# A graph layer's edge loop: first radial layer of two groups on two row groups of TensorE, and edge attributes copied by ScalarE into free columns of PSUM

## The reference

```python
h = jnp.maximum(_layernorm(x, axis=-1), 0.0)          # 6250 nodes x 160
l0, l1 = _fctp_scalar_attr(x0, x1, a, W_l1_0, W_l1_1)  # node table, gathered by src
r = jax.nn.relu(edge_length_embedded @ W_fc1 * (1.0 / np.sqrt(N_BASIS))) * RELU_GAIN  # 206250 x 10 -> 100
w = r @ W_fc2 * (1.0 / np.sqrt(N_RADIAL))              # -> w0 64, w1 64, w2 32, w3 32
y0 = l0[edge_src]; y1 = l1[edge_src]
e0 = edge_attr[:, :1]; e1 = edge_attr[:, 1:4]
m0 = w0 * y0 * e0
m1 = (w1 * y0)[:, :, None] * e1[:, None, :]
m2 = (w2 * e0)[:, :, None] * y1
m3 = w3 * jnp.einsum('eud,ed->eu', y1, e1) * INV_SQRT3
# sums of m0..m3 over the edges of each dst (sorted), W_l2_*, plus the node's own part, plus x
```

## Time and profile before

| | |
|---|---|
| median of 3 runs | 2946.77 us (2910.21 to 2948.76) |
| profiled execution | 2931.67 us |
| its span, first to last instruction | 2929.9 us |
| mean granted TensorE clock | 0.749 |
| TensorE matmuls busy | 2518.0 us |
| VectorE busy | 1661.1 us |
| GpSimd busy | 1617.6 us |
| ScalarE busy | 340.0 us |

### The profile page before, as it was taken

The page is one execution under the profiler, slowest core; times in us unless marked ns, Lnnn a source line. Parts: engine busy times, 40 slices in busy tenths (PEclk is TensorE's granted clock), DMA queues, the critical chain, the costliest instruction groups (busy, mean ns, idle before and its releaser), DMA issues.

```text
span 2929.9 us, 41982 instructions
## 1 busy us (share of the span) xinstructions
PE 2518.0 (86%) x11466; PEld 2003.8 (68%) x11466; DVE 1661.1 (57%) x4639; ACT 340.0 (12%) x636; POOL 1617.6 (55%) x1637
## 2 busy tenths in 40 slices
PE   6889888788989988888888888898888889898888
PEld 6667776667767766666666666676676677676677
DVE  5455656556656556555655555565565556556555
ACT  5000111011101011010101101010110111011111
POOL 4645555555655555545555554555465555555553
PEclk8566778787767687877777777777778777677876
DMA  4212222222222222212222221222122222222221
GB/s 132 58 45 52 54 55 54 51 53 53 56 50 55 53 52 56 52 47 55 50 53 50 54 55 48 52 51 56 46 60 51 50 52 54 50 55 52 51 53 36
DMA packets 160622, 158.30 MB, mean 54 GB/s; under 512 B 87570, under 2 KB 132534, under 8 KB 160602
## 3 DMA queue, kind: packets, MB, share of 16 engines
q0 software_dynamic: 77376, 132.16, 18.3%
q1 hardware_dynamic: 82088, 24.49, 3.7%
q10 hardware_dynamic: 1138, 1.43, 0.1%
HBM read 149.90 MB, written 8.03 MB: 54 GB/s over the span
## 4 chain that ended last, share of the span: by engine, by line
PE 57%; another core or an unknown queue 15%; DVE 13%; issue 10%; DVEq 4%; ACT 1%; DMA 0%; POOL 0%; ACTq 0%; SPq 0%; POOLq 0%
PE ps_w L894 16%; PE ps_s L922 14%; PE ps_s L924 12%; PE ps_h L887 11%; DVE hot L686 3%; DVEq L745 2%; DVE acc L742 2%; DVE dot L661 2%; DVE dots L656 2%; DVE msg L677 1%; DVE hot L680 1%; PE ps_s L910 1%; DVEq L742 1%; PE ps_s L906 1%
## 5 line engine op out<-in xcount | busy, mean ns | idle before, releaser
L381 POOL DMA_INDIRECT y<-table,idx x1612 | 1583.6, 982 | 1274.2 <-DVE msg L677 657.4
L894 PEld LDWEIGHTS ps_w<-w_fc,hr 100*128 100x128 f32 x3224 | 682.8, 241 | 456.9 <-issue 404.2
L894 PE MATMUL ps_w<-w_fc,hr 100*128 100x192 f32 x3224 | 839.2, 417 | 49.2 <-issue 26.8
L922 PE MATMUL ps_s<-hot,msg 128*128 128x128 f32 x3216 | 612.8, 346 | 136.5 <-DVE msg L677 84.9
L922 PEld LDWEIGHTS ps_s<-hot,msg 128*128 128x128 f32 x3216 | 569.3, 255 | 180.6 <-DVE msg L677 111.8
L742 DVE TENSOR_TENSOR acc<-acc,ps_s 64x32 f32 (+1 forms) x1612 | 327.1, 203 | 628.8 <-remote 346.7
L887 PE MATMUL ps_h<-rad,w_fc 10*100 10x512 f32 x806 | 556.8, 775 | 80.0 <-ACT hid_t L492 43.4
L924 PE MATMUL ps_s<-hot,msg 128*128 128x64 f32 x3216 | 531.6, 314 | 88.1 <-issue 87.7
L924 PEld LDWEIGHTS ps_s<-hot,msg 128*128 128x128 f32 x3216 | 521.0, 241 | 94.6 <-issue 94.2
L487 ACT ACTIVATE hr<-ps_h 100x512 f32<-100x512 f32 x403 | 239.3, 597 | 2409.4 <-remote 1012.6
L667 DVE TENSOR_TENSOR msg<-ps_w,y 128x512 f32<-128x512 f32 x404 | 278.9, 690 | 340.9 <-remote 163.9
(11 more groups left out here) (83 smaller groups left out, 537.4 us busy)
## 6 DMA issues: line engine op xcount, KB each, us to landing
y<-table,idx POOLq DMA_INDIRECT x1612
rad<-in_radial SPq DMA_DIRECT2D x202, 40.0 KB
xres<-in_x SPq DMA_DIRECT2D x7, 560.0 KB, 4.7
out<-xres SPq DMA_DIRECT2D x49, 80.0 KB
table<-y SPq DMA_DIRECT2D x6, 560.0 KB, 3.2
idx<-in_src SPq DMA_DIRECT2D x202, 4.0 KB
attr_sb<-in_attr SPq DMA_DIRECT2D x202, 16.0 KB
dst_i<-in_dst ACTq DMA_DIRECT2D x1, 808.0 KB, 7.2
```

The source lines that it names most:

```text
L381: nc.gpsimd.indirect_dma_start(out=y[:, j, t, :], out_offset=None, in_=table, in_offset=bass.IndirectOffsetOnAxis(ap=idx[:, j // HALF, col ...
L894: ins = nc.tensor.matmul(ps_w[:, s, t, 0:NW], hr[:, s, t * P:(t + 1) * P], w_fc2[:, :], start=True, stop=True)
L922: nc.tensor.matmul(ps_s[:, s, 0:4 * W], msg[:, s, t, 0:P], hot[:, s, t, 1:V, :], start=(t == 0), stop=(t == T - 1))
```

## The change

1. fc1 runs for two groups behind one another. `w_fc1` is loaded twice, at partitions 0 to 9 and 32 to 41; the host lays the basis values of each even group on partitions 0 to 9 and of the odd one on 32 to 41 (`radial_rows`, zeros between), so the two products use different row groups of the array. They write the two banks of `ps_h`. TensorE's order becomes, at even j: wait for the relu of g-1, fc1(g), fc1(g+1), fc2(g-1), windows(g-2); at odd j: fc2(g-1), windows(g-2).
2. ScalarE copies the 4 attributes of each edge of the group (128 x 16 elements) after each relu into columns 192 to 195 of `ps_w` (`move_attr`), after the messages of g-2. fc2(g) waits for the copy (the same PSUM banks). VectorE's dots and weigh read the attributes there, and so stand behind the waits for the copy and for fc2(g), which stood before `scalar_products`.
3. In a block's turn `turn_block` and `move_block` come at j = 3 instead of 2, and TensorE's wait for the moved block at j = 4 instead of 3.

```diff
-        w_fc1 = sb("w_fc1", [N_BASIS, N_RADIAL])
+        w_fc1 = sb("w_fc1", [ROW + N_BASIS, N_RADIAL])
-        rad = sb("rad", [N_BASIS, 2, HALF * GE])
+        rad = sb("rad", [ROW + N_BASIS, 2, GE])
+        def attr_behind(s, a, b, lo=0, hi=T):
+            return ps_w[:, s, lo:hi, NW + a:NW + b]
...
-                sp.dma_start(rad[:, c, :], radial[:, bass.ds(k * HALF * GE, HALF * GE)]).then_inc(ld_rad[c], 16)
+                sp.dma_start(rad[:, c, :], radial_rows[:, bass.ds(k * GE, GE)]).then_inc(ld_rad[c], 16)
...
+            def move_attr(i, j, first):
+                g, s = i * G + j, j % 2
+                if j % HALF == 0:
+                    act.wait_ge(ld_attr[j // HALF], i * 16 + 16)
+                if first:
+                    act.wait_ge(l_done, CHUNKS * NU)
+                else:
+                    act.wait_ge(msg_done, (g - 1) * 4)
+                nc.scalar.activation(attr_behind(s, 0, 4), attr_of(j, 0, 4), ACT.Copy).then_inc(attr_moved, 1)
...
                         relu(k * (2 * G) + j, j % 2, first and j < 2)
+                        move_attr(k * 2 + j // G, j % G, first and j < 2)
                         if finish and j == 1:
                             normalize(k - LAG, 0)
-                        if finish and j == 2:
+                        if finish and j == 3:
                             move_block(k - LAG, 0, 1)
-                        if finish and j == 3:
                             act.wait_ge(acc_done, k * (8 * G))
                             copy_block(k - LAG)
...
                 which(g, s)
                 dve.wait_ge(gathered[j], i * (16 * T) + 16 * T)
-                edge_dots(j)
-                weigh(g, j, s)
+                dve.wait_ge(attr_moved, g + 1)
+                dve.wait_ge(fc2_done, g + 1)
+                edge_dots(j, attr_behind(s, 1, 4))
+                weigh(g, s)
                 dve.wait_ge(dots_done, g + 1)
                 sum_dots()
-                dve.wait_ge(fc2_done, g + 1)
                 scalar_products(j, s)
...
-            def fc1(i, j):
-                if j % HALF == 0:
-                    pe.wait_ge(ld_rad[j // HALF], i * 16 + 16)
-                nc.tensor.matmul(ps_h[0:N_RADIAL, j % 2, 0:GE], w_fc1[:, :], rad[:, j // HALF, (j % HALF) * GE:(j % HALF + 1) * GE],
-                                 start=True, stop=True).then_inc(fc1_done, 1)
+            def fc1(i, c, some=HALF):
+                pe.wait_ge(ld_rad[c], i * 16 + 16)
+                for h in range(some):
+                    at = slice(h * ROW, h * ROW + N_BASIS)
+                    nc.tensor.matmul(ps_h[0:N_RADIAL, h, 0:GE], w_fc1[at, :], rad[at, c, :], start=True, stop=True).then_inc(fc1_done, 1)
             def fc2(g, s):
                 pe.wait_ge(relu_done, g + 1)
+                pe.wait_ge(attr_moved, g + 1)
...
-                        if finish and j == 3:
+                        if finish and j == 4:
                             pe.wait_ge(hidt_done, k - LAG + (CHUNKS * NU + 1))
-                        fc1(k * 2 + j // G, j % G)
+                        if j % HALF == 0:
+                            if not first or j:
+                                pe.wait_ge(relu_done, g)
+                            fc1(k * 2 + j // G, j % G // HALF)
...
-                        if finish and j == 2:
+                        if finish and j == 3:
+                            pe.wait_ge(relu_done, g + 1)
                             turn_block(k - LAG, 0, 1)
```

More of the change, by code:

```diff
@@ L49 @@
 ND = NP + P
+ROW = 32
 EPS = 1e-5
@@ L62, with gnn_layer @@
 AX = mybir.AxisListType
-def gnn_layer(nc, x, src, dst, radial, attr, avec, w_lin, w_lin_z, w_self, w_self_z, w_last, wf1, wf2, out):
+def gnn_layer(nc, x, src, dst, radial, radial_rows, attr, avec, w_lin, w_lin_z, w_self, w_self_z, w_last, wf1, wf2, out):
     ctx = ExitStack()
@@ L181, in gnn_layer @@
         hot_done = sem("hot_done")
+        attr_moved = sem("attr_moved")
         dots_done = sem("dots_done")
@@ L321, in general @@
                     sp.sem_inc(sp_passed, 1)
-                    sp.dma_start(rad[:, 0, 0:GE], radial[:, bass.ds(g * GE, GE)]).then_inc(g_loaded, 16)
+                    sp.dma_start(rad[0:N_BASIS, 0, :], radial[:, bass.ds(g * GE, GE)]).then_inc(g_loaded, 16)
                     sp.dma_start(idx[:, 0, 0:T], src[:, bass.ds(g * T, T)]).then_inc(g_loaded, 16)
@@ L432, in _ @@
             act.dma_start(w_out[:, :, :], w_last).then_inc(ld_w, 16)
-            act.dma_start(w_fc1[:, :], wf1).then_inc(ld_w, 16)
+            for h in range(HALF):
+                act.dma_start(w_fc1[h * ROW:h * ROW + N_BASIS, :], wf1).then_inc(ld_w, 16)
             act.dma_start(w_fc2[:, :], wf2).then_inc(ld_w, 16)
@@ L707, in last_messages @@
                 g, j, s = EDGE_GROUPS - 1, LEFT - 1, (EDGE_GROUPS - 1) % 2
-                if j % HALF == 0:
-                    dve.wait_ge(ld_attr[j // HALF], TURNS * 16)
                 which(g, s)
-                weigh(g, j, s)
+                dve.wait_ge(attr_moved, g + 1)
                 dve.wait_ge(fc2_done, g + 1)
+                weigh(g, s)
                 for h in range(2):
@@ L781, in general @@
                     dve.wait_ge(g_rows, g * (16 * T) + 16 * T)
[L782 removed]
+                    edge_dots(0, attr_of(0, 1, 4))
                     dve.drain()
@@ L947, in pair @@
                         g = k * (2 * G) + j
-                        if finish and j == 3:
+                        if finish and j == 4:
                             pe.wait_ge(hidt_done, k - LAG + (CHUNKS * NU + 1))
-                        fc1(k * 2 + j // G, j % G)
-                        if first and j == 1:
+                        if j % HALF == 0:
+                            if not first or j:
+                                pe.wait_ge(relu_done, g)
+                            fc1(k * 2 + j // G, j % G // HALF)
+                        if first and j == 0:
                             node_stage_left()
@@ L966, in windowed @@
                     g = (TURNS - 1) * G + j
-                    fc1(TURNS - 1, j)
+                    if j % HALF == 0:
+                        pe.wait_ge(relu_done, g)
+                        fc1(TURNS - 1, j // HALF, min(HALF, LEFT - j))
                     fc2(g - 1, (g - 1) % 2)
@@ L983, in general @@
                     pe.wait_ge(g_loaded, g * 48 + 48)
-                    nc.tensor.matmul(ps_h[0:N_RADIAL, 0, 0:GE], w_fc1[:, :], rad[:, 0, 0:GE], start=True, stop=True).then_inc(g_fc1, 1)
+                    nc.tensor.matmul(ps_h[0:N_RADIAL, 0, 0:GE], w_fc1[0:N_BASIS, :], rad[0:N_BASIS, 0, :], start=True, stop=True).then_inc(g_fc1, 1)
                     pe.wait_ge(g_relu, g + 1)
@@ L1031 @@
     radial[:, :E] = get["edge_attr_10"].T
+    radial_rows = np.zeros((ROW + N_BASIS, EP // HALF), np.float32)
+    for h in range(HALF):
+        radial_rows[h * ROW:h * ROW + N_BASIS] = radial.reshape(N_BASIS, -1, HALF, GE)[:, :, h].reshape(N_BASIS, -1)
     arrays = {
@@ L1036 @@
         "radial": radial,
+        "radial_rows": radial_rows,
         "attr": by_tile(get["edge_attr_4"], 0),
```

19 lines of the change are left out of this document (9 added, 10 removed).

## The result

The change makes the kernel slower by about 1.5%: 2979.94 us (median of 6 runs, 2962.69 to 2996.01) against 2947.77 us (6 runs, 2910.21 to 2956.69), ratio 1.0145, interval 1.0074 to 1.0216. The profiled execution took 2994.9 us, 63 more than that of before, at a mean granted clock of 0.715 instead of 0.749.

The account below looks back on a forecast made before the run. TensorE was the busiest engine (86%, 57% of the chain), with late signals an unexplained doubt. The sum was 2931.67 (profiled execution) - 80 (fc1) + 45 (VectorE behind fc2) = 2897 us, range 2775 to 3035.

Parts of the forecast that it names:

- the forecast's 2960: Upper end of the forecast's own case, 2830 to 2960 us around 2897; chance 0.36.
- the slower rival: VectorE's messages become the late step, 1.69 us paid at most of 154 late fc2: 2990 to 3110 us; chance 0.22.
- fc1, -80 us: TensorE's fc1 pair: only B1 runs beside A2, three slots of four, saving a quarter of fc1's 322 us chain share.
- the full overlap: Rival: an fc1 pair takes one fc1's time, -161 + 20 gives 2790 us, between 2740 and 2830; chance 0.16.
- the 100 us on the path: Sign: the forecast is wrong if relu's or accumulation's late waits, priced as unchanged, change by more than this on the path.
- VectorE behind fc2, +45 us: VectorE's dots, weigh and sum wait for fc2: 1.69 us paid in 27, half of 53 cases of windows waiting for messages.
- +140 us on the windows' wait: Sign: if TensorE's windows' wait for messages rises from 84.9 us by over 140, the slower rival is right.
- The copy, 0: ScalarE's 403 attribute copies, 0.3 us each, covered by 1.89 us of windows: price 0; uncovered 121 us.
- fc1 earlier, block turn, 0: The odd group's fc1 one slot sooner, new waits only for work issued a group earlier: between 0 and -10 us, taken 0.
- DMA, layout, PSUM reads, 0: Basis loads of 84 instead of 40 KB, 8.9 MB more, and VectorE reading attributes from PSUM: each priced at 0.
- the pace isn't the array's: Rival: time saved in fc1 comes back as waiting; 2931.67 us, between 2905 and 2960; chance 0.26.
- sign of equal waits for messages: Shorter pair, equal waits for messages and some 71 groups per 500 us would show the pace isn't the array's.

Follow-up runs that it names:

- half_cols: The kernel before with fc1 over 256 of its 512 columns (radial layer of half of the edges left out): 2961.28 us, 1.0041.
- pair_only: The kernel before with only the paired fc1 and the shifted block turn, attributes in SBUF, VectorE's order as before: 1.0195 on chip B, 1.0066 on chip D.
- dots_behind: The kernel before with one wait moved: VectorE waits for fc2 ahead of dots, weigh and sum: 1.0123 on chip B, 1.0107 on chip D.
- after_again: The whole changed kernel timed once more, on chip D against the kernel before: 2988.25 us, 1.0165.
- attr_only_2: The kernel before with only the attribute copy and the changed VectorE order, fc1 once per group, on the new basis layout: 3020.43 us, 1.0285 (chip D).
- copy_unread: The kernel before, on the new basis layout, plus the attribute copy and its waits; VectorE reads SBUF in its old order: 2863.33 us, 1.0092 (chip E).
- rows_only: The kernel before with only the 42-row basis layout, fc1 group by group on the two row groups by turns: 2942.43 us, 1.0003 (chip A).
- fc1_twice: The kernel before with every fc1 issued twice, on chip C, which has no late signals: 3012.09 us, 1.4222 against 2120.23 us.
- half_gathers: The kernel before with two of each group's four gathers left out, on chip C, which has no late signals: 1880.42 us, 0.8870.
- fewer_narrow: The kernel before with three of the four narrow window matmuls of each group left out: 2874.34 us, 0.9737 (chip A).

## Why the prediction was wrong

**The sign.** Forecast 2897 us; measured 2979.94, inside the range 2775 to 3035 but on the other side of before. It lies between the intervals of the rivals, above the forecast's 2960 and below the 2990 of the slower one: none of the four had a 1.5% loss in it.

**fc1, -80 us.** Two faults. The overlap was mis-sized: I took three slots of four from the order A1, A2, B1, B2. The passes start in the order A1, B1, A2, B2 and take two slots of four, at both clocks (1.04 and 1.96 us). The chain share fell from 322 to 0.05 x 2993 = 150 us, that is by 172, near the 161 of the full overlap. The Trainium skill's span formula (TensorE: Matmul & The Clock Gate, Part 3: Packing small matmuls) was right here. Its in-order rule isn't contradicted by these starts; what I had wrong was the order of the passes. The larger fault is the step from chain share to time. The share tells whose work the time was under, not what a shorter piece gives back: `half_cols` took 202 us out of fc1 and gained nothing, and `pair_only` lost 0.7% on D and 2.0% on B. The full overlap's 2790 us, in which I put +20 us without a reason, fell with the same step.

What came in its place is a wait that I had priced as unchanged, the late signals. Their share of the chain rose from 439 to 718 us in the change, and to 23% and 29% where fc1 alone is shorter. That is well over the 100 us on the path that I had named as the sign of a wrong forecast. Why a shorter fc1 brings more of them onto the path, and why the pair by itself costs time instead of nothing, stays open.

**VectorE behind fc2, +45 us.** The mechanism was right and is shown alone: `dots_behind` costs 1.1% (1.2% on B), 0.0107 x 2945.64 = 32 us, near the 45. Together with the shorter fc1 it is another matter: TensorE's waits for messages went from 108 to 315 us (to 359 in after_again), in the whole far more than either part makes (126 and 222). I had set +140 us on the windows' wait as the point where the slower rival is right; it rose by 100, with last_linear's by 193. I had not counted last_linear, which stands once in a pair behind the messages.

**The copy, 0.** Its duration (185 ns) is below my 0.3 us, and uncovered it is small: in the trace of attr_only_2 fc2 starts straight behind the copy some 25 times, at 0.17 us each about 4 us (an estimate). Yet `copy_unread` costs 0.9%, some 26 us. ScalarE now waits for messages there, with the next relu queued behind (120.1 us in 88 waits in copy_unread, 507.0 in after). I had called that relu wanted a group later. For copy_unread that held: in its trace no relu starts within 2.8 us of the end of a copy that had waited, so the queued relu doesn't explain the 26 us. In after 12 relus start straight behind such a copy. Where the 26 us come from stays open.

**fc1 earlier, block turn, 0.** The new wait ahead of turn_block takes 65.6 us in 20 cases, and that for the moved block fell from 43.4 to 12.9. Not tried alone; it lies in pair_only's 0.7%.

**DMA, layout, PSUM reads, 0.** Right: `rows_only` 1.0003; weigh 680 ns from PSUM (attr_only_2) against 685, dots 553 against 551.

**The rival "the pace isn't the array's".** Its reasoning held best: a shorter pair, 69 to 70 groups per 500 us, saved time back as waiting and as a lower clock. It lacked the loss, and its sign of equal waits for messages didn't come. I gave it 0.26 because nothing in the profile said what delays the signals; an argument that a fifth of the time is in neither clock state's period should have weighed more than a chain share.

No kernel here clearly beats the one before without leaving work out; on chips with late signals the change is best not made. On a chip without them it wasn't timed.

## What to carry to other kernels

A line's share of the chain isn't what a shorter line gives back. Leave half of the work out first, as `half_cols` did, and set the engine's busy time and idle time side by side (in the change 165 us less busy, 228 more idle). Where signals come late now and then, work that is moved behind such a signal can be paid each time (1.1% for one moved wait). A saving elsewhere didn't remove the late signals here; they took a larger share of the path. Time a change and its parts on the same chip: the parts' ratios differed by up to 1.3% between two chips.

## What the runs showed of the hardware

- One kernel took 2120 us on one chip and 2821 to 2948 on four others, its runs on one chip within 3% of each other; the bound changes with it (GpSimd's gathers on one, while late signals take 12% to 29% of the chain on the rest).
- A granted clock of 0.73 under a TensorE that is busy 100% of a 500-us stretch (`fc1_twice`), and 1.00 under another equally busy one (`half_gathers`). The Trainium skill (TensorE: Matmul & The Clock Gate, Part 1) ties a released clock to how busy the engine is; busy time alone doesn't give this difference.
- A lower mean clock isn't a longer time on A and D: `fewer_narrow` ran 2.6% faster at 0.605, and one run of the kernel before on D took 2913.60 us at 0.602 where its median is 2945.64 at 0.751.
- Four fp32 passes of 10 x 512 on two row groups take the time of two, at either clock level (1.04 and 1.96 us). They start in the order A1, B1, A2, B2, the two of a step 6 ns apart.
